# Fused attention and mixture-of-experts block on one core: scores in two row tiles, values in four bursts, and the surrounding work re-placed

## Time and profile before

| | |
|---|---|
| median of 3 runs | 811.04 us (810.09 to 813.9) |
| the profiled execution | 808.86 us |
| its span | 807.1 us |
| TensorE matmul busy | 92% |
| GpSimd busy | 77% |
| ScalarE busy | 75% |
| VectorE busy | 65% |
| mean granted TensorE clock | 0.992 of full speed |

### The profile page before, as it was taken

The page is one execution under the profiler, slowest core; times in us unless marked ns, Lnnn a source line. Parts: engine busy times, 40 slices in busy tenths (PEclk is TensorE's granted clock), DMA queues, the critical chain, the costliest instruction groups (busy, mean ns, idle before and its releaser), DMA issues.

```text
span 807.1 us, 19809 instructions
## 1 busy us (share of the span) xinstructions
PE 741.1 (92%) x5984; PEld 611.7 (76%) x5984; DVE 524.7 (65%) x1735; ACT 603.5 (75%) x1816; POOL 618.8 (77%) x842
## 2 busy tenths in 40 slices
PE   2568789999999999999999999999999999998876
PEld 1446668888887878787887878788887888787764
DVE  3466686767767676767667686767767685765232
ACT  4787788788787888878788788878787887864232
POOL 3426467879888888978888888988888887967876
PEclk9999999999999999999999999999999999999999
DMA  5000022040413213040313213040312204041331
GB/s 157 26 1 15 14 71 77 15 140 9 118 42 97 64 51 110 2 130 25 106 52 93 65 38 119 2 130 26 106 52 80 77 25 120 4 119 44 115 94 39
DMA packets 50738, 53.86 MB, mean 67 GB/s; under 512 B 5632, under 2 KB 31744, under 8 KB 50560
## 3 DMA queue, kind: packets, MB, share of 16 engines
q1 hardware_dynamic: 50688, 53.25, 22.2%
HBM read 44.31 MB, written 4.72 MB: 61 GB/s over the span
## 4 chain that ended last, share of the span: by engine, by line
PE 44%; ACT 19%; POOL 14%; issue 14%; DVE 5%; DMA 2%; POOLq 1%; SPq 1%; DVEq 0%; ACTq 0%
ACT probs L606 9%; PE PS L1057 8%; PE PS L873 7%; PE PS L983 7%; PE PS L915 6%; PE PS L874 5%; PE PS L875 5%; POOL gate L471 5%; ACT k_hi L530 3%; POOL hh L483 3%; POOL k_lo L463 2%; ACT th L564 2%; DVE neg_max L802 2%; PE PS L976 2%; PE PS L1054 2%
## 5 line engine op out<-in xcount | busy, mean ns | idle before, releaser
L606 ACT ACTIVATE probs<-PS,neg_max 128x96 f32<-128x96 f32 (+1 forms) x1024 | 244.5, 354 | 57.2 <-DVE neg_max L802 56.7
L471 POOL TENSOR_TENSOR gate<-gate,spread 128x512 f32<-128x512 f32 x128 | 164.4, 1285 | 63.2 <-DMA spread<-weights_by_expert 45.9
L754 DVE STREAM_TRANSPOSE probsT<-probs 128x384 f32<-128x384 f32 (+1 forms) x256 | 124.1, 523 | 101.9 <-ACT probs L606 101.9
L483 POOL TENSOR_TENSOR hh<-gate,tu 128x512 f32<-128x512 f32 x128 | 164.5, 1285 | 15.2 <-POOL gate L471 11.9
L790 DVE SCALAR_TENSOR_TENSOR tu<-th,PS 128x512 f32<-128x512 f32 x128 | 88.0, 687 | 94.2 <-PE PS L875 59.4
L1057 PE MATMUL PS<-wd,hh 128*128 128x128 f32 x1024 | 137.2, 277 | 10.1 <-POOL hh L483 10.0
L1057 PEld LDWEIGHTS PS<-wd,hh 128*128 128x128 f32 x1024 | 127.2, 193 | 16.2 <-POOL hh L483 8.1
L873 PE MATMUL PS<-x_hi,w_hi 128*128 128x512 f32 x288 | 125.7, 437 | 7.5 <-DVE tu L790 6.3
L802 DVE TENSOR_REDUCE neg_max<-PS 128x4 f32<-128x384 f32 (+1 forms) x256 | 125.3, 513 | 8.4 <-PE PS L983 5.6
L564 ACT ACTIVATE th<-PS 128x512 f32<-128x512 f32 x128 | 80.0, 625 | 63.6 <-PE PS L875 63.6
L875 PE MATMUL PS<-x_lo,w_hi 128*128 128x512 f32 x288 | 114.3, 397 | 0.0
(11 more groups left out here) (108 smaller groups left out, 1363.8 us busy)
## 6 DMA issues: line engine op xcount, KB each, us to landing
spread<-weights_by_expert SPq DMA_DIRECT2D x256, 128.0 KB, 3.0
X<-x SPq DMA_DIRECT2D x32, 256.0 KB, 3.6
OUT<-H SPq DMA_DIRECT2D x16, 256.0 KB, 3.0
out<-OUT SPq DMA_DIRECT2D x16, 256.0 KB, 3.1
probsT<-w_gu SPq DMA_DIRECT2D x1, 1152.0 KB, 8.2
wd<-w_down SPq DMA_DIRECT2D x1, 512.0 KB, 8.6
weights_by_expert<-cT SPq DMA_DIRECT2D x16, 32.0 KB, 1.6
probsT<-w_att SPq DMA_DIRECT2D x1, 264.0 KB, 3.7
```

The source lines that it names most:

```text
L471: tt(gate2[:, :], gate[:, k % 2, :], spread[:, k % SP_BUFS, :], ALU.mult).then_inc(s_g2, 1)
L483: tt(hh[:, k % 2, :], gate2[:, :], tu[:, k % 2, :], ALU.mult).then_inc(s_h, 1)
L606: ins = nc.scalar.activation(probs[:, u % 2, tt, a, j0:KW], PS[:, tt, a * KW + j0:a * KW + KW], ACT.Exp, bias=neg_max[:, tt, a:a + 1])
L754: ins = v_.transpose(probsT[:, b, :, t0 + tt, c0:3, :].rearrange("p g c q -> p g (c q)"), probs[:, u % 2, tt, :, c0 * Q:KW])
```

## The change

- **Scores.** The contraction is split into two row tiles of 64 rows, rows 0 to 63 writing PSUM bank 0 and rows 64 to 127 bank 1. Queries and keys are kept in plain float32, queries in four copies by head (`q_by_head`), keys in two (`k_by_row`), both double-buffered by group. Per unit there are two mask matmuls (four in units 0 and 4) and four float32 matmuls of up to 192 columns, instead of two and six of up to 384. All of a unit's scores wait for all exponentials of the unit before.
- **Copies.** The high and low splits of q and k, the GpSimd and VectorE instructions for them and their semaphores are gone. ScalarE writes four q copies (128x512 each) and two k copies (128x512) straight from PSUM, with a per-partition scale. K is projected in one piece.
- **Stages.** LN1 moves from stage 0 to 3, XT from 1 to 4, QP from 2 to 5, KP to 6, VP from 5 to 6, VB from 6 to 7. The values are multiplied in four bursts (stages 12, 13, 16, 17) of 16 matmuls each, not eight of 8.
- **Transposes** of the probabilities: one VectorE instruction per unit, not two.
- **Loop** over slots 4 to 15.
- **Weights.** The feed-forward weights are loaded into a tile of their own and split into high and low parts by GpSimd in slot 1; GpSimd also writes the ones beside the values. ScalarE and VectorE did this in slot 0.
- **Drain.** In slots 16 to 19 `hh` is formed by VectorE, after its other work of the step, not by GpSimd.

```diff
-LN1 = 0
-XT = 1
-QP, VP, VB = 2, 5, 6
-QC = (4, 8)
-QC_LOW = (4, 9)
-KP = (6, 8)
-KC = (7, 10)
-KC_LOW = (7, 11)
+LN1 = 3
+XT = 4
+QP, KP, VP, VB = 5, 6, 6, 7
-PV = 11
+PV = (12, 13, 16, 17)
...
-LOOP_FIRST, LOOP_END = 6, NG
+LOOP_FIRST, LOOP_END = 4, NG
...
+def draining(slot):
+
+    return slot.fixed and slot.n >= NG
...
-LOADS, FFN_LOADS = 4, 4
+LOADS, FFN_LOADS = 4, 6
...
+        q_by_head = sb("q_by_head", [P, 2, NSB, 4, Q])
+        k_by_row = sb("k_by_row", [P, 2, 2, TOK])
+        queryrow = sb("queryrow", [P, 4])
+        keyrow = sb("keyrow", [P, 2])
...
+                    if sl.fixed and sl.n == 1 and s == PREPARE:
+                        pool.wait_ge(s_wf, 16 * FFN_LOADS)
                         nc.gpsimd.tensor_scalar(bias2[:, :], bias_b[:, :], 2.0, 1.0, ALU.mult,
                                                 ALU.add).then_inc(s_pool, 1)
+                        nc.gpsimd.tensor_scalar(w_hi[:, GK:W_COLS], ffn_stage[:, :], 1.0, 0.0, ALU.mult,
+                                                ALU.add).then_inc(s_cst, 1)
...
+                        tt(w_lo[:, GK:W_COLS], ffn_stage[:, :], w_hi[:, GK:W_COLS].bitcast(F32),
+                           ALU.subtract).then_inc(s_cst, 1)
...
+                        for par in range(2):
+                            ones = headcol.unsqueeze(1).broadcast_to([P, NSB * HG, 32])
+                            tt(v_bd[:, par, :, :, 1, :].rearrange("p n g f -> p (n g) f"), ones, ones,
+                               ALU.mult).then_inc(s_ones, 1)
...
-                        for a in (2 * pair_, 2 * pair_ + 1):
-                            tt(q_lo[:, NQ * b:NQ * b + NQ, a, :], blocks(qr_lo[:, T * b:T * b + T].bitcast(F32)),
-                               grouprow[:, a:a + 1].unsqueeze(2).broadcast_to([P, NQ, Q]), ALU.mult).then_inc(s_q_lo, 1)
...
-                            for a in range(HG):
-                                tt(k_lo[:, a, T * b:T * b + T], kr_lo[:, :].bitcast(F32),
-                                   headrow[:, a:a + 1].broadcast_to([P, T]), ALU.mult).then_inc(s_k_lo, 1)
...
                     g, k = at(sl, s, FF, 1, NP)
-                    if g:
+                    if g and not draining(sl):
                         pool.wait_ge(s_g2, g.n * NP + k + 1)
                         pool.wait_ge(s_tu, g.n * NF + k + 2)
                         tt(hh[:, k % 2, :], gate2[:, :], tu[:, k % 2, :], ALU.mult).then_inc(s_h, 1)
...
-                        copy(qr_hi[:, :], bank, scale=Q_SCALE).then_inc(s_high[side], 1)
...
+                    g, _ = at(sl, s, QP)
+                    if g:
+                        if g.fixed and g.n == 0:
+                            act.wait_ge(s_pool, 7)
+                        side, bank = filled(act, sl, s, LATE)
+                        for v in range(4):
+                            ins = copy(q_by_head[:, g.par, :, v, :], blocks(bank), scale=queryrow[:, v:v + 1])
+                        ins.then_inc(s_taken[side], 1)
+                    g, _ = at(sl, s, KP)
+                    if g:
+                        side, bank = filled(act, sl, s, LATE)
+                        for e in range(2):
+                            ins = copy(k_by_row[:, g.par, e, :], bank, scale=keyrow[:, e:e + 1])
+                        ins.then_inc(s_taken[side], 1)
...
-                        for tt in range(2):
-                            ins = v_.transpose(
-                                probsT[:, b, :, t0 + tt, c0:3, :].rearrange("p g c q -> p g (c q)"),
-                                probs[:, u % 2, tt, :, c0 * Q:KW])
-                        ins.then_inc(s_pt, 1)
+                        v_.transpose(probsT[:, b, :, t0:t0 + 2, c0:3, :].rearrange("p g t c q -> p t g (c q)"),
+                                     probs[:, u % 2, :, :, c0 * Q:KW]).then_inc(s_pt, 1)
...
+                    g, k = at(sl, s, FF, 1, NP)
+                    if g and draining(sl):
+                        dve.wait_ge(s_g2, g.n * NP + k + 1)
+                        dve.wait_ge(s_tu, g.n * NF + k + 2)
+                        v_.tensor_tensor(hh[:, k % 2, :], gate2[:, :], tu[:, k % 2, :], ALU.mult).then_inc(s_h, 1)
...
-                        pe.wait_ge(s_pt, g.n * NU + 4 * b + min(p + 1, 3) + 1)
-                        for kb in (2 * p, 2 * p + 1):
+                        pe.wait_ge(s_pt, g.n * NU + 4 * b + (4 if later else 3))
+                        for kb in range(4 * later, 4 * later + 4):
...
+                        if not (g.fixed and g.n == 0 and u == 0):
+                            pe.wait_ge(s_p, 2 * (g.n * NU + u))
+                        quarters = [slice(64 * rows, 64 * rows + 64) for rows in range(2)]
...
                         for tt in range(2):
-                            if not (g.fixed and g.n == 0 and u == 0):
-                                pe.wait_ge(s_p, 2 * (g.n * NU + u) + tt - 1)
...
-                            for ql, kl in ((q_hi, k_hi), (q_lo, k_hi), (q_hi, k_lo)):
+                            for rows, r in enumerate(quarters):
+                                dst = PS[:, rows, 2 * KW * tt:2 * KW * tt + 2 * KW].rearrange("p (e k) -> p e k", e=2)
                                 ins = mm(dst[:, :, KW - nk:KW],
-                                         ql[:, q1 // Q - 1, :, :].rearrange("p v q -> p (v q)"),
-                                         kl[:, :, q1 - nk:q1], start=False, stop=(kl is k_lo), skip_group_check=True)
-                            ins.then_inc(s_s, 1)
+                                         q_by_head[r, g.par, q1 // Q - 1, :, :].rearrange("p v q -> p (v q)"),
+                                         k_by_row[r, g.par, :, q1 - nk:q1], start=False, stop=(tt == 1),
+                                         skip_group_check=True)
+                                if tt == 1:
+                                    ins.then_inc(s_s, 1)
```

More of the change, by code:

```diff
@@ L582, in slot @@
                         nc.scalar.activation(th[:, :], PS[:, 4, :], ACT.Tanh, scale=0.5).then_inc(s_th, 1)
-                    keys(1)
-                    g, _ = at(sl, s, QP)
-                    if g:
-                        if not (g.fixed and g.n == 0):
-                            act.wait_ge(s_q_hi, g.n * GB)
-                        side, bank = filled(act, sl, s, LATE)
-                        copy(qr_hi[:, :], bank, scale=Q_SCALE).then_inc(s_high[side], 1)
                     g, _ = at(sl, s, XT)
@@ L732, in slot @@
                 for s in range(STEPS):
-                    if sl.fixed and sl.n == 0 and s == 1:
+                    if sl.fixed and sl.n == 0 and s == LN1 + 1:
                         dve.wait_ge(s_w, 16 * LOADS)
@@ L839, in slot @@
                                                 ALU.mult).then_inc(s_tu, 1)
-                    keys(1)
-                    g, _ = at(sl, s, QP)
-                    if g:
-                        if not (g.fixed and g.n == 0):
-                            dve.wait_ge(s_q_lo, g.n * 8)
-                        side, bank = high_out(sl, s, LATE)
-                        v_.scalar_tensor_tensor(qr_lo[:, :], bank, Q_SCALE, qr_hi[:, :].bitcast(F32),
-                                                ALU.mult, ALU.subtract).then_inc(s_taken[side], 1)
                     g, _ = at(sl, s, XT)
@@ L918, in slot @@
                                          start=(kb == 0 and a < 2), stop=(kb == NQ - 1), skip_group_check=True)
-                        if p == 3:
+                        if later:
                             ins.then_inc(s_o_ps, 1)
@@ L968, in slot, with hide @@
-                        j0 = Q if u % 4 == 0 else 0
+                            taken(pe, slot_before(sl), QP % STEPS, LATE)
+                            taken(pe, slot_before(sl), KP % STEPS, LATE)
+                        if not (g.fixed and g.n == 0 and u == 0):
+                            pe.wait_ge(s_p, 2 * (g.n * NU + u))
+                        quarters = [slice(64 * rows, 64 * rows + 64) for rows in range(2)]
+                        def hide(n0, n1, which, first, step, start):
+                            for rows, r in enumerate(quarters):
+                                dst = PS[:, rows, 0:4 * KW].rearrange("p (n k) -> p n k", n=4)[:, n0:n1, :]
+                                hidden = slice(first, KW // Q, step)
+                                mm(blocks3(dst)[:, :, hidden, :], ident4[r, :],
+                                   blocks2(band[r, which, :])[:, hidden, :].unsqueeze(1).broadcast_to(
+                                       [64, n1 - n0, len(range(3)[hidden]), Q]),
+                                   start=start, stop=False, skip_group_check=True)
@@ L969, in slot @@
+                        if u % 4 == 0:
+                            hide(0, 2, 1, 1, 1, True)
+                            hide(2, 4, 0, 2, 1, False)
+                        else:
+                            hide(0, 4, 0, 0, 2, True)
                         for tt in range(2):
```

(13 more changed lines are left out.)

184 lines of the change are left out of this document (46 added, 138 removed).

## The result

The changed kernel takes 791.43 us (median of 4 runs, 790.12 to 793.12), the kernel before 810.57 beside it: a ratio of 0.9757, 95% interval 0.9721 to 0.9794. The prediction was 796 us. The total came out near it, but the way there did not: the steady slots gave time back that I had said they would cost, and the drain gave little.

What follows compares the result with a forecast made beforehand. TensorE was taken to bound most of a slot, a VectorE and ScalarE chain the rest. Terms -8.3 - 2.5 + 5.5 - 2 - 7 = -14.3 on 808.86 gave 794.6, plus 2.2 for the median: 796 us, range 766 to 814.

Steps and rivals of the forecast that it cites:

- the steady slots: The repeating middle slots: each goes from 45.7 to 46.2 us, over 11 slots +5.5 us.
- Scores: A unit's scores on TensorE: 1.04 us instead of 1.32 with overlapping row tiles, bounds 0.85 and 1.66.
- TensorE's work: TensorE's busy time per slot: falls by 2.9 us, to about 42 of 45.2 us.
- Stretch A: Slot from scores of step 1 to shared expert in step 3: 13.24 us becomes 12.7, bounds 12.2 and 13.3.
- Stretch B: Slot from shared expert to the next step 1, bound by TensorE: 32.46 us grows by 1.2 to 33.6.
- LN1 ahead of `tu`: Layer norm 1's statistics in step 3: 1.25 us of VectorE work that `tu` and TensorE's shared expert wait for.
- Start: Start of the kernel: first scores at 16.9 us against 24.78, -8.3 after slot 1, slots 2 and 3 about -2.5.
- Slot 16: First slot without the next group's layer norm and projections: 44.3 us becomes 42.3, so -2.
- Drain: Last slots, with `hh` on VectorE: 2.5 us a step instead of 2.9 and shorter waits, -7 (bounds -2 and -10).
- TensorE bounds everywhere: Rival: the stretch before the shared expert shrinks with TensorE's work, slot 43.5 us, time 766; chance 0.22.
- Row tiles do not overlap: Rival: a unit's scores take 1.66 us, 2.6 more per slot, time 828; chance 0.12.
- ScalarE and VectorE are later: Rival: first stretch stays 13.2 us and step 6 waits 1.1, slot 47.3, time 808; chance 0.21.

Runs made afterwards that it cites:

- the second trace: The changed kernel run and traced again with no edit: 791.95 us, ratio 0.9788 to the kernel before.
- same_rows: The changed kernel with both halves of a unit's scores computed from rows 0 to 63, so no row tiles can overlap: 853.13 us.
- pv_eight: The changed kernel with the values multiplied in eight bursts again, one per unit: 776.6 us, ratio 0.9587 to the kernel before.
- pv8_hh_last: The changed kernel with the values in eight bursts and `hh` on VectorE in slot 19 alone: 778.33 us, ratio 0.962 to the kernel before.

## Why the prediction was right or wrong

**The number** was right within its range, and that it came so near was luck: the forecast had 11 us too much for the steady slots, 8 too little for slot 16 and the drain, and 1.4 too little for the start (11, 6.4 and 2.4 by the second trace), which nearly cancel. A slip of one more is in the last line, 794.6 + 2.2 being 796.8.

**Scores.** Taken at 1.04 us a unit with the change of tiling ahead of it, measured 0.87 + 0.09 = 0.96 (the 0.09: 448.80 to 449.12, less the 0.23 of a matmul). The bounds, 0.85 and 1.66, are both seen now, the upper one as 1.62 in `same_rows`. The way to the value, by the row it is nearest to, worked. The Trainium skill (TensorEngine Tiling (Array Packing), Key Properties) says that different tiles can load and multiply in parallel; for row tiles this case now agrees, with 0.87 us per unit against 1.62.

**TensorE's work** was to fall to about 42 us per slot: 42.36. Merging the bursts was to save 1.1 us of it and saves 1.13 (43.49 - 42.36).

**Stretch A** is the step that failed: 12.7 predicted, 11.21 measured. VectorE's work was right (10.8, measured 10.55). The waits between it were not. Of 2.41 us I struck only routing's 1.1; that and the joined transposes make 12.0, and the rest of my 12.7 had no term. Two more waits went, of `tu` on ScalarE's `th`, which had stood behind copies that the change removes. ScalarE and VectorE of the kernel before, step 2:

```profile
420.82 0.96 ACT L530 ACTIVATE q_hi<-qr_hi,cst 128x256 fp32r<-128x256 f32 x2
421.62 0.65 ACT L564 ACTIVATE th<-PS 128x512 f32<-128x512 f32 x1
422.31 0.69 DVE L790 SCALAR_TENSOR_TENSOR tu<-th,PS 128x512 f32<-128x512 f32 x1 [0.55 <-ACT th L564]
```

In step 3 the same wait is 0.16 us, behind four `k_hi` copies. In the kernel after neither is there, and ScalarE has 7.81 us of work in A instead of 11.07. 13.24 - 1.11 - 0.55 - 0.16 and 0.28 less work of VectorE give 11.14. So the sentence that failed is the one on the copies of GpSimd and ScalarE, "none of it is on either path". This is read from waits; no run puts the copies back. What can be ruled out is that A shrank because scores come sooner or TensorE has room: in `same_rows` a unit takes 1.62 us and TensorE has 11.09 us of work in A, and A is 11.29; the 11.23 of `pv_eight` show that four bursts have no part in it. My lower bound, 12.2, was too high: the chain closed up to within 0.7 us of VectorE's work.

**Stretch B**: 33.6 predicted, 33.96 measured. The +0.70 for bursts moved out of A (measured 0.80) and the wait of step 6 (0.5, measured 0.71) were the right terms. I wrote that the room in A "is waste" and did not draw the conclusion that the bursts should have stayed there.

**LN1 ahead of `tu`**: the statistics, taken as 1.25 us, do stand in front of `tu`, from 413.20 to 414.37 in the kernel after (1.17), and TensorE's wait is 1.23 (1.5 forecast). The waits before the scores of steps 2 and 3 are 0.55 and 0.33, not over 1. But taking them away brings 0.56 us a slot with four bursts and costs 0.49 with eight.

**Start**: first scores at 16.9 predicted, 18.53 measured. I let the projections run through; the K product waits 1.30 us for ScalarE's query copies to free its bank, and so the chain is product, copies, product, copies. Group 1 then follows 34.2 us later (35 taken).

**Slot 16**: -2 predicted, -0.1 measured. The 44.3 us that I started from are 43.7 from `OUT` to `OUT`. With eight bursts it is 42.53 us (680.19 - 637.66), as the 42.3 of the prediction: the other 1.1 us are what four bursts cost here too.

**Drain**: -7 predicted, -0.5 measured (-2.5 in the second trace). The pace in slot 19 was right (2.5 us a pair; in `pv_eight` (769.96 - 759.62) / 4 = 2.6 between the gates of GpSimd). What failed is the sentence on VectorE's queue, "no new bound, but close": I priced `hh` there by its 0.69 us and by pairs, and not by what stands behind it while it waits for `gate` (17.7 us of such waits). That this alone makes the missing 4.5 to 6.5 us is not shown.

**Rivals.** "TensorE bounds everywhere" had A shrink to 9.9 us with TensorE's work. A did shrink, but to VectorE's work and not to TensorE's, and `same_rows` and `pv_eight` show that it does not follow TensorE's. The 44.09 of `pv_eight` come near the rival's 43.5 by another way. "Row tiles do not overlap" fell by `same_rows`. Of "ScalarE and VectorE are later" only the 0.7 us of step 6 came.

## What to carry to other kernels

Before you merge or move work to save an engine its overhead, ask which engine bounds the stretch that the work leaves and the one that it enters: the same edit (eight bursts to four) took 0.34 us from a slot where TensorE was the bound in both stretches and added 1.08 where it had room in the one left. Work taken off an engine that is not the bound can still be worth its time: ask what stood behind it (here `th` behind the `q_hi` copies). When work is moved on an engine that executes in the order written, price the move by everything that queues behind it, on GpSimd's and ScalarE's queues too: layer norm's statistics had three places, and each made another engine late. A wait that the profile puts down to one releaser may need two; swap their order in thought first.

## What the runs showed of the hardware

- Row tiles: eight float32 instructions of 192 columns in two row tiles take 0.87 us with their masks, the same eight in one row tile 1.62, so the tiles overlap almost wholly.
- Changes of tiling: eight matmuls of 128 columns take 0.99 us ahead of a burst of `v_bd` and 0.81 otherwise (434.91 to 435.72 in the kernel after), and the first of 512 columns behind a burst 0.33 instead of 0.23.
- With the scores in one row tile, TensorE was granted 0.61 of its clock from 80 to 110 us of the start while it was busy 29.96 of 30 us; with two row tiles, and less busy (24.54), it had 0.83. A busy TensorE is no sign of a full clock.
- Nor does a slot's share of busy time tell its clock: slot 18 of `pv_eight` was granted 0.85 with TensorE busy 28.94 of 34.14 us, slot 19 of `pv8_hh_last` 1.00 with 19.93 of 24.98.
- The pace of equal matmuls shows the level directly: those of 512 columns follow each other in 0.23 us in the steady slots and in 0.43 behind the wait at 766.40. They also do at the start of the kernel after (11.80 to 12.23), where the windows' clock reads 1.00.
- The lower clock came and went between two executions of the same kernel: slot 19 was 22.19 us at 0.92 and 20.61 at 1.00. A difference of 2 us in a drain is no measure of an edit from one trace of each kernel.
